# A mixture-of-experts stage cut into 20 tiles of four 32-token blocks, and the first pair's sums moved ahead of later time steps

## The reference

```python
h = tok(word, modality, segment, npi, position ids, age_tau, delays_tau)  # four table rows summed
#     plus sin(tau * w + b) and one linear column, for two taus; then a layer norm
h = h + attn(layernorm(h))     # 12 heads of 16, q and k normalised by their root mean square
h = h + ffn(layernorm(h))      # one of 16 experts per token
# ffn: normed = rms_norm(x); expert = argmax(softmax(normed @ w_router))
#   at most 64 tokens of one sequence go to one expert; a token that finds no place keeps `normed`
#   y = relu(normed @ wi[expert]) @ wo[expert]      (192 -> 768 -> 192)
#   out = x + router_prob * y
```

## Time and profile before

| | |
|---|---|
| median of 3 runs | 377.9 us (377.55 to 379.37) |
| the profiled execution's own time | 379.93 us |
| its span in the trace | 378.2 us |
| busy: PE, DVE, ACT, POOL | 336.9, 257.6, 161.0, 200.0 us |
| PE busy between 260 and 360 us | 100.0 of 100 us |
| first and last `hidden` start | 236.69, 359.29 us (24 tiles) |

### The profile page before, as it was taken

How to read it: one execution, slowest core, us unless ns; L and a number is a source line. 1 busy time by engine, 2 the same in 40 slices (tenths; PEclk the granted TensorE clock), 3 DMA queues, 4 the chain that set the end, 5 groups by cost and what they waited for, 6 DMA issues and landing times.

```text
span 378.2 us, 8634 instructions
## 1 busy us (share of the span) xinstructions
PE 336.9 (89%) x3180; PEld 218.6 (58%) x3194; DVE 257.6 (68%) x740; ACT 161.0 (43%) x300; POOL 200.0 (53%) x191
## 2 busy tenths in 40 slices
PE   8999698799899999899999725999999999999970
PEld 3545566576677776577776412455655566556640
DVE  7688766855979799986677777666656655665520
ACT  2556244524466655466555220333434343333320
POOL 5778741785476741045101356456676667666321
PEclk9999699956999999999999977999999999999996
DMA  3436920325629780453333480593211221122100
GB/s 79 116 87 178 302 74 1 76 45 102 158 34 216 184 205 18 148 166 86 107 100 91 131 247 21 135 298 97 56 54 48 54 59 54 42 54 60 30 3 0
DMA packets 35066, 37.96 MB, mean 100 GB/s; under 512 B 6214, under 2 KB 32531, under 8 KB 35022
## 3 DMA queue, kind: packets, MB, share of 16 engines
q1 hardware_dynamic: 25680, 24.20, 22.2%
q0 software_dynamic: 8768, 12.63, 15.1%
q10 hardware_dynamic: 576, 0.59, 0.5%
HBM read 30.97 MB, written 7.21 MB: 101 GB/s over the span
## 4 chain that ended last, share of the span: by engine, by line
PE 66%; DVE 19%; issue 5%; DMA 4%; ACT 2%; POOL 1%; DVEq 0%; POOLq 0%; ACTq 0%
PE psum L1500 12%; PE psum L1479 8%; PE psum L1243 6%; PE psum L1457 6%; PE psum L1244 5%; PE psum L1484 5%; PE psum L1491 4%; PE psum L1299 4%; PE psum L1380 3%; PE psum L1313 3%; DMA shared<-token_rows,blk_token 3%; DVE small L844 2%; PE psum L1471 1%; PE psum L1237 1%; PE psum L1452 1%
## 5 line engine op out<-in xcount | busy, mean ns | idle before, releaser
L1188 DVE COPY shared<-weights 128x1152 f32 x96 | 69.2, 765 | 10.5 <-issue 10.3
L529 POOL DMA_INDIRECT tower_out<-shared,oidx x24 | 36.2, 1508 | 35.9 <-DVE shared L1202 33.3
L1500 PE MATMUL psum<-shared 128*64 128x192 f32 x576 | 52.1, 330 | 0.9 <-ACT shared L722 0.9
L1500 PEld LDWEIGHTS psum<-shared 128*64 128x64 f32 x576 | 39.2, 137 | 19.4 <-issue 13.8
L1202 DVE SCALAR_TENSOR_TENSOR shared<-psum,shared 128x192 f32<-128x192 f32 x24 | 10.0, 418 | 46.1 <-PE psum L1500 46.1
L1479 PE MATMUL psum<-shared 128*64 128x384 f32 x192 | 36.3, 499 | 0.5 <-ACT shared L714 0.5
L718 ACT ACTIVATE shared<-psum 128x768 f32<-128x768 f32 x24 | 19.5, 812 | 36.4 <-PE psum L1484 36.4
L1243 PE MATMUL psum<-shared,weights 96*128 96x192 f32 (+1 forms) x96 | 33.5, 432 | 0.7 <-ACT weights L581 0.7
L925 DVE TENSOR_REDUCE guard<-psum 128x12 bf16<-128x1536 f32 x16 | 28.1, 1755 | 7.5 <-PE psum L1299 7.5
L522 POOL DMA_INDIRECT shared<-token_rows,blk_token x24 | 26.2, 1093 | 11.3 <-issue 6.0
L437 POOL TENSOR_TENSOR small<-small,mhalf 128x2 f32<-128x2 f32 x16 | 12.1, 758 | 36.9 <-DVE small L852 36.8
(11 more groups left out here) (197 smaller groups left out, 700.6 us busy)
## 6 DMA issues: line engine op xcount, KB each, us to landing
weights<-in_wo SPq DMA_DIRECT2D x16, 576.0 KB, 6.9
weights<-in_wi SPq DMA_DIRECT2D x32, 192.0 KB, 4.4
weights<-in_wi SPq DMA_DIRECT2D x32, 96.0 KB, 4.6
token_rows<-shared SPq DMA_DIRECT2D x14, 192.5 KB, 2.6
tower_out<-shared SPq DMA_DIRECT2D x14, 96.0 KB, 2.9
token_rows<-shared ACTq DMA_DIRECT2D x2, 192.5 KB, 3.2
blk_token<-expert_lists,blk_entry POOLq DMA_INDIRECT x24, 2.4
shared<-token_rows,blk_token POOLq DMA_INDIRECT x24, 3.4
```

The source lines that it names most:

```text
L529: G.indirect_dma_start(out=out, out_offset=bass.IndirectOffsetOnAxis(ap=oidx[q % 2][:, :], axis=0), in_=res[q % 2], in_offset=None, bounds ...
L1188: V.tensor_copy(w_now[q % 2][k][:, lo:hi], weights[:, bass.ds(at[k] + lo, hi - lo)]).then_inc(sem(("wi_now", "wo_now")[part]), 1)
L1500: last = T.matmul(psum[q % 2][k * BT:(k + 1) * BT, 3, 0:D], hidT[:, c * P + k * BT:c * P + (k + 1) * BT], w_now[q % 2][k][:, WI_COLS + c * ...
```

## The change

Four things. (1) A block has 32 tokens, a tile four blocks, and there are 20 tiles (2048 / 32 + 16 = 80 blocks). A matmul of the expert part then has 32 stationary columns rather than 64, and there are twice as many of them in a tile. (2) `w_now` has one set of four blocks rather than two sets of two. DVE copies blocks 0 to 2, ACT copies block 3 (`take_last`); a copy of `wi` for tile q waits until `hidden(q-1)` is done, one of `wo` until `output(q-1)` is done. DVE reads the three columns for tile q+2 between the `wi` copies of tile q+1 and the `wo` copies of tile q. (3) The plan's work area moves from `shared` into the place of expert 12 in `weights`; so SP loads expert 12 only after the plan's last step, and DVE copies all of tile 0's weights ahead of the plan's last ten steps. (4) On PE six of the eight time steps stay ahead of the turns; steps 6 and 7 are inside turn 1. On DVE the first pair's `plain_rows` and `es` come ahead of the fractions 4 to 7.

```diff
-BT = P // 2
+NB = 4
+BT = P // NB
-NTILE = NBLK // 2
+NTILE = NBLK // NB
...
-        w_now = [[share_b(WCOL) for _ in range(2)] for _ in range(2)]
+        w_now = [share_b(WCOL) for _ in range(NB)]
...
-        plan = shared[:, 5888:6288]
+        plan_room = carver(weights, 12 * WCOL, 13 * WCOL)
+        plan = plan_room(400)
...
-            sp.wait_ge(sem("rows2"), 16)
-            for e in (12, NE - 2, NE - 1):
-                load_expert(e)
+            sp.wait_ge(sem("rows0"), 16)
+            sp.wait_ge(sem("plan"), N_PLAN)
+            load_expert(12)
+            sp.wait_ge(sem("rows1"), 16)
+            load_expert(NE - 2)
+            load_expert(NE - 1)
...
+            def take_last(q, part):
+                lo, hi = ((0, WI_COLS), (WI_COLS, WCOL))[part]
+                freed(act, sem(("b_hid", "b_y")[part]), q)
+                for e in range(max(NB * q, ARENA_FIRST), min(NB * q + NB, NE)):
+                    act.wait_ge(sem(f"weights{e}"), 80)
+                S.copy(w_now[NB - 1][:, lo:hi], weights[:, bass.ds(last_at[q % 2] + lo, hi - lo)]).then_inc(
+                    sem(("wi_last", "wo_last")[part]), 1)
...
             for q in range(NTILE):
                 if q + 1 < NTILE:
+                    last_at[(q + 1) % 2] = last_column(q + 1)
+                    take_last(q + 1, 0)
                     turn_rows(q + 1)
                 turn_hid(q)
+                if q >= 1:
+                    take_last(q, 1)
                 if q + 1 < NTILE:
                     relu(q + 1)
...
             for q in range(NTILE):
                 if q + 1 < NTILE:
-                    at = columns(q + 1)
-                    take_weights(q + 1, 0)
+                    take_weights(q + 1, 0, (0, 1, 2))
+                if q + 2 < NTILE:
+                    at[(q + 2) % 3] = columns(q + 2)
                 if q >= 1:
+                    take_weights(q, 1, (0, 1, 2))
                     result(q - 1)
-                if q + 1 < NTILE:
-                    take_weights(q + 1, 1)
...
                 for b in range(2):
-                    for k in range(2):
+                    for k in range(NB):
                         T.matmul(hid_ps[k * BT:(k + 1) * BT, b, :], gT[:, b * P + k * BT:b * P + (k + 1) * BT],
-                                 w_now[q % 2][k][:, b * WI2:(b + 1) * WI2], start=True, stop=False)
+                                 w_now[k][:, b * WI2:(b + 1) * WI2], start=True, stop=False)
...
             add_times(2)
-            fraction(4)
-            add_times(3)
             plain_rows(0)
             es(0)
+            fraction(4)
             ed(0)
             st2(0)
+            add_times(3)
+            sh2(0)
             fraction(5)
-            sh2(0)
-            fraction(6)
-            fraction(7)
             add_times(4)
             constants()
             scale_in()
             plain_rows(1)
+            fraction(6)
```

More of the change, by code:

```diff
@@ L67, in tower_kernel @@
 def tower_kernel(nc, t, out):
-    assert NBLK == 48 and NTILE == 24
+    assert NBLK == 80 and NTILE == 20
     ctx = ExitStack()
@@ L647, in act_turn @@
             def act_turn(t):
+                if t == 2:
+                    sines(7)
+                    S.activation(cols(small[1], ZSUM + 1, 1), round_up[:, 0:1], ACT.Exp, scale=0.0)
                 if live(t - 3):
@@ L679, in act_turn @@
                 if t == 1:
-                    sines(7)
-                    S.activation(cols(small[1], ZSUM + 1, 1), round_up[:, 0:1], ACT.Exp, scale=0.0)
+                    sines(6)
+                    rounded(7)
                 if live(t - 2):
@@ L828, in constants @@
                 V.tensor_scalar(low_half[:, :], token_iota[:, 0:1], float(BT), None, ALU.is_ge).then_inc(sem("halves"), 1)
-                dve.wait_ge(sem("halves"), 1)
+                for k in range(1, NB - 1):
+                    dve.wait_ge(sem("halves"), k)
+                    V.scalar_tensor_tensor(low_half[:, :], token_iota[:, 0:1], float((k + 1) * BT), low_half[:, :], ALU.is_ge, ALU.add).then_inc(sem("halves"), 1)
+                dve.wait_ge(sem("halves"), NB - 1)
                 V.scalar_tensor_tensor(half_pos[:, :], low_half[:, :], -float(BT), token_iota[:, 0:1], ALU.mult, ALU.add).then_inc(sem("halves"), 1)
@@ L1071, in dve_turn @@
                 if t == 2:
+                    fraction(7)
                     add_times(5)
@@ L1155, in _ @@
             dve.wait_ge(sem("bases"), NSEQ + 1)
-            dve.wait_ge(sem("halves"), 6)
-            big, big2 = (shared[:, 4608 + 512 * k:4608 + 512 * k + NTILE * NE].rearrange("p (j e) -> p j e", e=NE) for k in range(2))
+            dve.wait_ge(sem("halves"), 8)
+            big, big2 = (plan_room(NTILE * NE).rearrange("p (j e) -> p j e", e=NE) for k in range(2))
             nb, cum, spare = (cols(plan, a, NE) for a in (16, 32, 48))
             nth, ej, within, length, late = (cols(plan, 112 + 32 * a, NTILE) for a in range(5))
-            over_k = shared[:, 5632:5632 + NE * SPLIT].rearrange("p (e k) -> p e k", k=SPLIT)
+            over_k = plan_room(NE * SPLIT).rearrange("p (e k) -> p e k", k=SPLIT)
             def over(v):
@@ L1380, in keep, with times @@
                     T.matmul(bank, warm16[:, 0:P], warm16[:, :], start=True, stop=True)
+            def times(p):
+                freed(pe, sem("linear"), p - 2)
+                for u, n in seqs(p):
+                    last = T.matmul(time_ps[p][:, u, 0:2 * D + 1], tau_rows[0:4, n * P:(n + 1) * P], time_w[0:4, :], start=True, stop=True)
+                last.then_inc(sem("p_time"), 1)
             def pe_turn(t):
@@ L1402, in pe_turn @@
                     tx(t - 1)
+                if t == 1:
+                    times(6)
                 if t == 10:
@@ L1435, in pe_turn @@
                 if t == 1:
-                    pe.wait_ge(sem("linear"), NPAIR)
-                    keep(psum_m[0], 6)
+                    times(7)
+                    pe.wait_ge(sem("linear"), NPAIR - 1)
+                    keep(psum_s[:, 0, :], 6)
                 if live(t - 1):
@@ L1453, in _ @@
             pe.wait_ge(sem("time_w"), 2)
[L1454 to L1457, removed]
-                last.then_inc(sem("p_time"), 1)
+            for p in range(6):
+                times(p)
             pe.wait_ge(sem("ident"), 8)
```

68 lines of the change are left out of this document (40 added, 28 removed).

## The result

| | before | changed |
|---|---|---|
| median | 378.06 us (377.55 to 379.37, 4 runs) | 366.98 us (366.41 to 371.94, 4 runs) |
| ratio | | 0.968 (95% interval 0.9637 to 0.9722) |
| span of the profiled execution | 378.2 us | 364.7 us |
| first `hidden` starts, last one ends | 236.69, 361.61 us (24 tiles) | 236.29, 347.83 us (20 tiles) |

What follows compares the result with a forecast made beforehand. PE bounded the expert loop before; DVE was to set 5.6 us tiles after. `hidden(3)` at 264.1, later tiles to 354.3, the end 372.1, front -0.6: span 371.5, 6.7 shorter, so median 371.2 us (8 in 10: 365.5 to 380).

Steps and rivals of the forecast that it cites:

- PE in a tile: Expert loop: four blocks of 32 columns run side by side, so PE's tile stays 5.37 us, upper end 6.3.
- the rival of four blocks not side by side: Expert loop: PE's work does not shrink, 65 us more, about 443 us; chance 0.03.
- DVE in a tile: Expert loop: six copies and three column reads on DVE exceed PE's work and set the tile at 5.6 us.
- ACT in a tile: Expert loop: with a 1.12 us weight copy and a column read, ACT needs 5.17 us, under 5.6, so charged nothing.
- POOL: Expert loop: POOL's three DMAs a tile take at most 5.1 us, under 5.6, so charged nothing.
- the rival: Copies of tiles 4 to 19: DVE and POOL exclude each other, tile 6.9 us, 392 us (381.6 at half effect); chance 0.13.
- Tile 3: New wait for experts 12 to 15: `hidden(3)` ends 5.9 us later, plus 2.2 for PE's slower clock, at 264.1.
- The end: After the last `hidden` (354.3): 16.7 us as before plus 1.1 for ACT's `wo` copy, span ending at 372.1.
- The front: Ahead of the first turns: earlier sums on DVE and fewer PE steps bring -0.6 us (bounds +2 to -1.5).
- the first: Expert loop: PE stays the bound, period 5.4, clock does not fall at tile 3; about 365.8 us, chance 0.17.
- The third: After tile 3: PE's clock stays at 1.2 GHz, 17 us at half speed cost 8.5; 377.5 us, chance 0.09.
- the signs: Trace signs for the forecast: tiles 5.6 us apart, PE idle 5 to 7 us before tile 3, clock 0.5, `tx` near 29.4.

Runs made afterwards that it cites:

- e4: Changed kernel with DVE reading a fourth, unused column per tile: 375.19 us, ratio 0.993 to the kernel before.
- e3: Changed kernel with a tile's three DVE column reads ahead of the `wi` copies instead of behind them: 389.10 us, ratio 1.029 to the kernel before.
- e13: Changed kernel with two POOL multiplications of 256 columns after each tile's scatter, into columns nobody reads: 389.79 us, ratio 1.023 to the kernel before.
- e2: Changed kernel with 32 filler matmuls on PE between the hid turns of tile 2 and `hidden` of tile 3: 367.28 us, ratio 0.970 to the kernel before.
- The two experiments: The change's front alone put into the kernel before: 379.51 us, ratio 1.001; the changed kernel without its front: 367.17 us, ratio 0.971.
- e10: Changed kernel without the change's front (old order on PE, DVE and ACT): 367.17 us, ratio 0.971 to the kernel before.
- e1: Changed kernel with experts 14 and 15 loaded right after the last routing logits, 12 still after the plan: 363.18 us, ratio 0.960 to the kernel before.
- e11: Changed kernel with expert 14 loaded right after the last routing logits, 15 after the first rows, 12 after the plan: 360.48 us, ratio 0.951.
- e8: Changed kernel with experts 14 and 15 both loaded once the last list scatter has landed, 12 after the plan: 367.44 us, ratio 0.969.
- e6: Changed kernel with expert 14 loaded after the last list scatter, 15 after the first rows, 12 after the plan: 363.57 us, ratio 0.960.

## Why the prediction came out as it did

- **PE in a tile**: right. 5.37 us were taken, 5.34 came, and the upper end (6.3) fell with the rival of four blocks not side by side.
- **DVE in a tile**: here the prediction failed, in the step "With nothing beside them two reads took 1.91 us, so one is 0.95", which charged a third read with the mean of two. A further read costs about 0.6 (0.58 in e4, 0.61 at the plan). The trace of before shows the read itself, a `TENSOR_LOAD` of 521 ns in the median at L1192. The first `wi` copy to the first `wo` copy is 2.53 us and not 2.88, DVE needs about 5.12 and not 5.43 to 5.97 (the 5.57 is also 0.02 over its own terms), and PE stays the bound. That the reads hide under the copies, and cost 1.5 us a tile where they don't, was right (e3).
- **ACT in a tile**: right. Its copy takes 1.15 us (1.12 taken). Its column read was charged with DVE's 0.95; the `TENSOR_LOAD` alone, at L753, takes 278 ns in the median.
- **POOL**: right, and e13 points to why the rival did not come: POOL's operations in the loop only issue DMAs. Beside them DVE's copies stay about as they were (776 ns in the mean from 270 to 350, 765 before), and only POOL's side is longer (the scatter 971 ns at best, 1374 in the median); beside POOL's arithmetic the copies are 1.0 us longer for three. The Trainium skill, "SBUF — State Buffer", section "SBUF: two separate sides", lets the two exclude each other for a whole instruction; for DMA issues the trace shows the one side alone. The arithmetic in e13 loses time on both sides, but less than that would have it: two multiplications took 1.54 us with no copy beside them and three copies 2.10, and together they lie within 3.26 us (290.29 to 293.55), not 3.64.
- **Tile 3**: right in kind. The plan ended at 238.73, not 240.3: the first read began 0.7 us earlier, the six reads ahead of it, mis-sized in the same way, took 0.7 less, and the copies and the ten steps 0.2 less. The loads needed 8.8 us of SP as forecast, and the last one 7.5 to land, not 8.1. So `hidden(3)` ended at 261.5, 2.6 us before the 264.1 forecast. The clock cost 1.95 us on `hidden`, forecast 2.2, and 0.53 on `output`, which was not forecast. The 0.6 us of tile 4 were swallowed by the slow `hidden`; e2 shows them.
- **The end**: the last `hidden` ends 16.9 us ahead of the span's end, forecast 17.8. The term of 1.1 us was right: the last `output` starts at 352.86, just behind the end of ACT's `wo` copy (352.61), and 5.10 us after the `output` before it, where before it was 3.86 (361.54 to 365.40). But the span ends 8.4 us after the last scatter starts (356.30), where before it was 9.4 (368.84). Why, stays open.
- **The front**: -0.6 was forecast. The two experiments put it within about 1.3 us of nothing; its sign stays open.
- **The sum**: the forecast, 371.2, is 4.2 us over the measured 367.0. 16 x (5.6 - 5.34) is 4.2 too, but that is chance. The forecast of the span, 371.5, missed the trace's 364.7 by 6.8: 3.9 from tiles 4 to 19, 2.6 from the earlier end of `hidden(3)`, 0.9 from the end, less the 0.6 that was taken off for the front. Of the 6.8 the median shows only 4.2, since the traced execution before was 2.0 over the median that the forecast started from and the traced one of the change 0.6 under its own.
- Of the rivals, the first was half right: PE stays the bound, and its 365.8 us is nearer than the forecast. But it paired that with a clock that does not fall, and the clock fell. The third did not come: from 265 to 270 the granted clock is 1.00 again.
- Of the signs, the idle stretch before tile 3 (5.36 us), the clock of 0.50 behind it and the first turn of x near 29.4 (29.52) came. Tiles 5.6 us apart did not, and the turn of x tells nothing, as e10 has it with the old order.

## What to carry to other kernels

A register read costs little where enough work is queued ahead of it on the same engine and its full time where none is: here the same three reads made a tile 1.5 us longer or nothing. When a loop is shortened, look at what it now asks for sooner: 7.9 of the 22.0 us that fewer tiles gave went into a wait for weights that were early enough for tiles of two blocks, and into the slow clock behind it. And before moving such a load up, look at which small, late-bound transfer it will stand in front of.

## What the runs showed of the hardware

- Weights ahead of a small transfer delay it by several us: 2.4 MB made the list scatter land 3.7 us later (e1), 1.2 MB 1.9 (e11), of which 0.2 and 0.7 lie ahead of it, in the attention. The row gather behind both loads kept PE idle for 6.79 us (e8).
- PE's clock is part of the price of a wait: a `hidden` takes 4.25 us at granted clock 0.50 and 2.30 at 1.00, behind the stall of tile 3 and at the first tile of e6 alike (4.25 us in both). Matmuls of no use hold it at 1.00 through a wait of 5.4 us (e2), which by itself won 1.7 us in the trace and nothing that the medians could show.
- One execution's start of the attention is not another's: with the same code up to there, the transposes of the third pair started between 70.4 and 72.3 us. A term of 0.6 us in the front can't be read from a single trace.
- A column read on DVE costs about 0.6 us more for each further one, in its `TENSOR_LOAD` 0.52 us in the median; three of them beside queued copies left no idle time on PE (79.87 of 80 us busy), and ahead of the copies they cost 2.02 us of DVE's time in a tile (e3).
